# Small tensors allocated behind the large ones, so that every large matmul operand starts at a multiple of 256 bytes of SBUF

## The chip, the cores and the metric

One core of one Trainium2 chip runs the whole program in one launch. The metric is device time in microseconds, the median of a few runs; lower is better.

## What is computed

A decoder of two layers on x (2 sequences of 512 tokens, 512 features, float32), with a context of 2 x 1024 x 512. Each of six steps is a layer norm, a block, and an addition to the residual stream:

```python
x = x + L0_attn(ln(x))                  # causal self-attention, 16 heads of 32
x = x + L0_xattn(ln(x), ctx, mask)      # softmax(x ctx^T) ctx over 1024 context rows, no weights
x = x + L0_ffn(ln(x))                   # 16 experts, 6 per token, gated, inner 352; 2 shared
x = x + L1_attn(ln(x))                  # RMS norm, rotary, 32 query heads of 64 in 8 groups
x = x + L1_xattn(ln(x), ctx, ctx, ones) # linear attention: relu features, 16 heads
x = x + L1_ffn(ln(x))                   # 8 experts, 2 per token, inner 352; 1 shared
```

## The kernel before

**Stages.** `program` runs six stages in this order: `Attention` a0 (0 to about 255 us in the profile), `Memory` m (to 375), `Mixture` f0 (to 960), `Attention` a1 (to 1520), `Linear` lin (to 1780) and `Mixture` f1. Each has a method per engine (`sp`, `pool`, `act`, `dve`, `pe`) that writes that engine's instructions out by hand, with semaphore waits between them; no scheduler reorders anything.

**Precision.** A float32 product is made of three float32r matmuls. Each operand is kept as a high part and a low part (names end in H and L), and `product` (L147 to 155) issues high·high, high·low and low·high into one PSUM bank. So nearly all matmuls have one line, L153, and are told apart by their tiles: `bank<-YL,a_WH` has the stationary operand a_WH and the moving operand YL.

```python
for j, (a, b) in enumerate(((lh, rh), (lh, rl), (ll, rh))):
    m = pe.matmul(out, a, b, ...)   # a: stationary, up to 128 columns; b: moving, up to 512 columns
```

**The matmuls with 512 moving columns**, on which the prediction turns (stationary, then moving):

- a0 and a1, Q/K/V projections: weights `WH`/`WL`, normed activations `k.YH`/`k.YL` (12 in a row for each product of four blocks); output projection: `QH`/`QL` (attention's output), `WH`/`WL`; scores of a1 (L1000): `QH`/`QL`, `KH`/`KL`; attention times values: `VH`/`VL`, `PH`/`PL` (tile `PHL`).
- m, scores: `YH`/`YL`, context `CH`/`CL`; readout: `PH`/`PL`, context rows `RH`/`RL`.
- f0 and f1, down projection (`_pe_down`): hidden `HH`/`HL`, weights `DH`/`DL`, nine a row tile.
- lin, keys: `W1`, `CH`/`CL`; values: `CH`/`CL`, `W2`; queries: `W1`, `YH`/`YL`; query features: `F`, `KH`/`KL`; output: `kfH`/`kfL`, `W2`.

The up projections of f0 and f1 have 352 moving columns (`XH`/`XL` or `YH`/`YL` stationary, `UH`/`UL` moving), key features of lin 256 (`F` moving), and the rest of a1 and a0 128 to 384.

**Where tensors lie.** `k.sb` (L143) opens an SBUF tensor. Tensors are placed one behind the other in the order of the calls, each rounded up to 32 bytes of every partition; the first begins at byte 16512. Those of `program` and `constants` stay for good, those of a stage are closed by its `end`, and the next stage starts again at the same byte. Small tensors between large ones therefore set the start of all that follow. The slices that a matmul takes begin at multiples of 512 bytes (of 1408 in the up projections) from the tile's start, so with 512 columns an operand's start modulo 256 is that of its tile.

Of the kernel before, what the change touches and what calls it, by code (L numbers as in the profile page):

```python
# [6 lines left out]
F32R = mybir.dt.float32r  # L7
BF16 = mybir.dt.bfloat16
# [6 lines left out]
P = 128  # L15
B, T, D = 2, 512, 512
NTOK = B * T
NT = NTOK // P
TT = T // P
KD = D // P  # L20
SC = 1024
CT = SC // P
# [46 lines left out]
class Kernel:  # L69
# [18 lines left out]
    def constants(self, t):  # L88
# [3 lines left out]
        self.upto, self.full, self.number = self.sb("upto", [16, 16]), self.sb("full", [7]), self.sb("number", [64])  # L92
# [50 lines left out]
    def sb(self, name, shape, dt=F32, scope=None):  # L143
        return (scope or self.ctx).enter_context(self.nc.sbuf_tensor(name, [P] + list(shape), dt))
# [266 lines left out]
class Attention:  # L411
# [15 lines left out]
    def __init__(self, k, name, w_qkv, w_out, heads, qtiles, hd, rotary=None, rms=None):  # L427
# [4 lines left out]
        sb = lambda nm, shape, dt=F32: k.sb(f"{name}_{nm}", shape, dt, s)  # L432
# [13 lines left out]
        self.top, self.total, self.inv = (sb(x, [self.SLOTS, 4]) for x in ("top", "total", "inv"))  # L446
        self.f, self.g = ([sb(f"{x}{i}", [T], F32R)[:, :] for i in range(2)] for x in "fg")
        self.causal = sb("causal", [T], BF16)
        if rotary is None:
            self.zeros = sb("zeros", [D])  # L450
        self.norm = Norm(k, name, lambda nm, shape: sb(f"n_{nm}", shape),
# [598 lines left out]
class Memory:  # L1050
# [6 lines left out]
    def __init__(self, k, ctxT, ctx_rows, mask):  # L1057
# [3 lines left out]
        sb = lambda nm, shape, dt=F32: k.sb(f"m_{nm}", shape, dt, s)  # L1061
# [4 lines left out]
        self.mb, self.valid, self.ones = sb("mb", [B, SC], BF16), sb("valid", [B]), sb("ones", [P], BF16)  # L1066
        self.E = [sb(f"E{i}", [SC]) for i in range(2)]
        self.PH, self.PL = [sb(f"PH{i}", [SC], F32R) for i in range(2)], [sb(f"PL{i}", [SC], F32R) for i in range(2)]
        self.top, self.total = sb("top", [NT, 2]), sb("total", [NT, 2])
        self.nb, self.inv = sb("nb", [NT]), sb("inv", [NT])  # L1070
        self.norm = Norm(k, "m", lambda nm, shape: sb(f"n_{nm}", shape), banks=list(range(NT)))
# [283 lines left out]
class Mixture:  # L1355
# [13 lines left out]
    def __init__(self, k, name, w_up, w_down, routed, shared, gated, router, bias, top, freed, turn, apart=0):  # L1369
# [4 lines left out]
        sb = lambda nm, shape, dt=F32: k.sb(f"{name}_{nm}", shape, dt, s)  # L1374
# [16 lines left out]
        self.XH, self.XL = sb("XH", [KD, P], F32R), sb("XL", [KD, P], F32R)  # L1391
        self.gate = sb("gate", [INNER])
        self.HH, self.HL = sb("HH", [3, P], F32R), sb("HL", [3, P], F32R)
# [894 lines left out]
class Linear:  # L2288
# [4 lines left out]
    HN, HD, FD = 16, 32, 64  # L2293
    G, VA, NP = P // 32, 33, 8
    PAIRS = {5: (0, 1, 2), 6: (3, 4, 5), 7: (6, 7)}

    def __init__(self, k, t, free):
        self.k, self.t, self.free = k, t, free
        HN, HD, FD, VA, NP = self.HN, self.HD, self.FD, self.VA, self.NP
        self.scope = s = ExitStack()  # L2300
        sb = lambda nm, shape, dt=F32: k.sb(f"lin_{nm}", shape, dt, s)
# [10 lines left out]
        self.bq, self.bk, self.bv, self.bo = sb("bq", [KD]), sb("bk", [KD]), sb("bv", [D]), sb("bo", [D])  # L2312
        self.am = sb("am", [CT])
# [3 lines left out]
        self.kfH, self.kfL = ([sb(f"kf{x}{i}", [HN * FD], F32R) for i in range(2)] for x in "HL")  # L2317
        self.v = sb("v", [HN, VA])
        self.vHL = [sb(f"vHL{i}", [2, HN, VA], F32R) for i in range(2)]
        self.acc = sb("acc", [B * NP, 2 * VA])  # L2320
        self.zerob = sb("zerob", [3 * 4 * VA], BF16)
        self.kvH, self.kvL = sb("kvH", [B * NP, 2 * VA], F32R), sb("kvL", [B * NP, 2 * VA], F32R)
# [540 lines left out]
def program(nc, t):  # L2863
    with ExitStack() as ctx:
        k = Kernel(nc, t, ctx)
        k.X, k.stats = k.sb("X", [NT, D]), k.sb("stats", [NT, 6])
# [135 lines left out]
```

## Time and profile before

| what | value |
|---|---|
| median of 3 runs | 1956.21 us (1951.85 to 1958.1) |
| the profiled execution, first to last instruction (the page gives no other time of it) | 1968.5 us |
| its mean granted TensorE clock | 0.966 |
| busy: PE, PEld, DVE, ACT, POOL | 93%, 81%, 56%, 40%, 51% |
| chain that ended last: PE | 55% of the span |

PE is TensorE's matmuls, PEld its weight loads, which run beside the matmuls. Matmuls overlap: a row's duration is from issue to the modelled end, so a row of 390 ns can be followed by the next start after 230 ns. The spacing of the starts is what a matmul costs when PE is never idle. The granted clock is given as a share of full speed: 1.00 is the level of 2.4 GHz, 0.50 that of 1.2 GHz.

### The profile page before, as it was taken

How to read it: one execution, taken by the hardware profiler on the slowest of the kernel's cores; microseconds unless marked ns; L12 is line 12 of the kernel's file. 1: busy time of each engine (PE TensorE's matmuls, PEld its weight loads, DVE VectorE, ACT ScalarE, POOL GpSimd, SP SyncE). 2: the span in 40 equal slices, each digit the busy share in tenths (PEclk: the TensorE clock that was granted, in tenths of full speed). 3: DMA queues.
4: the chain of work that ended last, by engine and by line, in shares of the span. 5: the costliest groups of instructions: out<-in, count | busy, mean ns of one | idle time of the engine just before them, and what ended most of it. 6: DMA issues, size and time to landing. Idle time of an engine off the chain costs nothing.

```text
span 1968.5 us, 30804 instructions
## 1 busy us (share of the span) xinstructions
PE 1831.7 (93%) x10221; PEld 1597.7 (81%) x10221; DVE 1109.8 (56%) x2771; ACT 787.8 (40%) x2024; POOL 1008.5 (51%) x960
## 2 busy tenths in 40 slices
PE   7999989999899999999779999999999999998896
PEld 5888857778799999898568888888887888887785
DVE  5676785663333333336657666666665766445344
ACT  3766633212122222221356666666563433223231
POOL 3444342487864867885356456455443113016783
PEclk8999999999999999999889999999999999889898
DMA  3556431156554645553243233332331110012565
GB/s 110 164 159 199 136 134 44 46 183 229 190 177 127 212 153 181 173 162 107 73 104 102 67 90 95 85 90 66 93 100 39 34 49 22 1 45 95 191 209 187
DMA packets 102694, 232.33 MB, mean 118 GB/s; under 512 B 18816, under 2 KB 19072, under 8 KB 99472
## 3 DMA queue, kind: packets, MB, share of 16 engines
q1 hardware_dynamic: 82224, 144.11, 24.6%
q0 software_dynamic: 19744, 85.47, 13.2%
q8 instruction: 90, 1.47, 0.3%
q10 hardware_dynamic: 576, 0.79, 0.2%
q14 instruction: 60, 0.49, 0.1%
HBM read 126.23 MB, written 57.93 MB: 94 GB/s over the span
## 4 chain that ended last, share of the span: by engine, by line
PE 55%; POOL 5%; DVE 4%; issue 3%; DMA 3%; SPq 3%; ACT 2%; another core or an unknown queue 1%; POOLq 0%; DVEq 0%; ACTq 0%
PE bank L153 45%; PE bank L1016 2%; PE bank L1000 2%; SPq L669 2%; PE bank L2178 2%; DMA a_g<-a_f 2%; PE bank L2169 2%; POOL a_g L700 1%; DMA a_QL<-a_g 1%; POOL f_UL L165 1%; POOL a_E L706 1%; SPq L654 1%; PE bank L2788 1%; DVE X L1884 1%
## 5 line engine op out<-in xcount | busy, mean ns | idle before, releaser
L706 POOL TENSOR_SCALAR a_E<-a_E,a_inv 128x128 f32<-128x128 f32 (+3 forms) x384 | 220.5, 592 | 224.4 <-DVE a_inv L842 224.4
L153 PE MATMUL bank<-f_UH,f_XH 128*128 x596 | 201.7, 339 | 20.5 <-issue 11.6
L739 ACT ACTIVATE a_E<-a_E,a_top 128x512 f32<-128x512 f32 (+3 forms) x384 | 211.1, 567 | 6.5 <-DVE a_top L836 6.4
L153 PE MATMUL bank<-f_UH,f_XL 128*128 x596 | 193.9, 325 | 0.0
L153 PE MATMUL bank<-f_UL,f_XH 128*128 x596 | 193.7, 325 | 0.0
L731 ACT ACTIVATE a_PHL<-bank 128x512 fp32r<-128x512 f32 (+1 forms) x288 | 130.7, 528 | 133.5 <-PE bank L1016 133.4
L153 PE MATMUL bank<-a_PHL,a_VH 128*128 128x512 f32 (+3 forms) x768 | 180.8, 324 | 0.3 <-DVE a_QL L165 0.3
L836 DVE CUSTOM_DVE_ANT_0 a_E<-a_causal,bank 128x512 f32<-128x512 bf16 (+3 forms) x384 | 163.7, 481 | 29.9 <-PE bank L1000 18.2
L165 DVE TENSOR_TENSOR a_PHL<-bank,a_PHL 128x512 fp32r<-128x512 f32 (+1 forms) x288 | 153.7, 587 | 11.3 <-ACT a_PHL L731 11.1
L1772 ACT ACTIVATE f_HH<-bank 128x256 fp32r<-128x256 f32 x220 | 59.9, 325 | 240.5 <-PE bank L2169 217.3
L1827 DVE TENSOR_TENSOR f_gate<-bank,f_gate 128x352 f32<-128x352 f32 x79 | 41.3, 523 | 201.3 <-PE bank L153 172.2
L700 POOL TENSOR_TENSOR a_g<-a_g,a_cos_sin 128x512 f32<-128x512 f32 x40 | 70.7, 1768 | 158.1 <-DMA a_g<-a_f 158.1
L153 PE MATMUL bank<-f_DH,f_HH 128*128 (+1 forms) x330 | 139.5, 423 | 9.2 <-issue 6.2
L153 PEld LDWEIGHTS bank<-a_PHL,a_VH 128*128 128x128 f32 x768 | 134.8, 189 | 15.1 <-DVE a_QL L165 0.6
L165 POOL TENSOR_TENSOR f_UL<-f_uraw,f_UH 128x2816 fp32r<-128x2816 f32 (+1 forms) x27 | 141.5, 5241 | 2.3
L1016 PE MATMUL bank<-ident,a_E 128*128 128x128 f32 x960 | 126.3, 275 | 15.1 <-DVE a_PHL L165 9.5
L153 PE MATMUL bank<-YH,a_WH 128*128 128x512 f32 x288 | 123.3, 428 | 11.7 <-ACT a_f L809 7.2
L153 PEld LDWEIGHTS bank<-f_UH,f_XH 128*128 128x128 f32 x596 | 113.7, 191 | 23.1 <-issue 23.1
L153 PE MATMUL bank<-f_DH,f_HL 128*128 (+1 forms) x330 | 132.1, 400 | 0.0
L153 PE MATMUL bank<-f_DL,f_HH 128*128 (+1 forms) x330 | 131.3, 398 | 0.0
L165 POOL TENSOR_TENSOR f_DL<-f_draw,f_DH 128x1024 fp32r<-128x1024 f32 (+1 forms) x54 | 98.2, 1836 | 62.9 <-DVE f_row L217 60.8
L1016 PEld LDWEIGHTS bank<-ident,a_E 128*128 128x128 f32 x960 | 106.9, 141 | 22.1 <-DVE a_PHL L165 12.0
(397 smaller groups left out, 4951.4 us busy)
## 6 DMA issues: line engine op xcount, KB each, us to landing
f_uraw<-f_up POOLq DMA_DIRECT2D x18, 1408.0 KB
f_xb<-table SPq DMA_DIRECT2D x86, 256.0 KB
table<-f_ob SPq DMA_DIRECT2D x86, 256.0 KB
table<-a_zeros SPq DMA_DIRECT2D x31, 512.0 KB, 4.5
f_draw<-f_down POOLq DMA_DIRECT2D x27, 512.0 KB
a_g<-a_f SPq DMA_DIRECT2D x160, 64.0 KB, 2.0
a_raw<-a_qkv SPq DMA_DIRECT2D x36, 256.0 KB, 3.2
f_uraw<-f_up POOLq DMA_DIRECT2D x9, 704.0 KB
```

Source lines behind the costliest of these rows:

```text
L153: m = pe.matmul(out, a, b, start=first and i == 0 and j == 0, stop=last and i == n - 1 and j == 2, skip_group_check=not check)
L165: return dve.tensor_tensor(lo, src, hi, ALU.subtract)
L669: e.dma_start(self.g[s][32 * i:32 * i + 32, :].bitcast(F32), self.f[s][32 * (i ^ 1):32 * (i ^ 1) + 32, :].bitcast(F32)).then_inc(*self.s_t ...
L700: e.tensor_tensor(g, g, self.cos_sin[:, 1, :], ALU.mult).then_inc(*self.s_p2.up(N, *x))
L706: e.tensor_scalar(self.E[sl][:, a], self.E[sl][:, a], self.inv[:, sl, i:i + 1], 0.0, ALU.mult, ALU.add).then_inc(*self.s_nrm.up(N, m - 1, i))
L731: e.activation(self.PH[m % 2][:, at:at + size], bank[:, 0:size], ACT.Copy).then_inc(*self.s_phi.up(N, m - 2, ci))
L739: x = e.activation(E, E, ACT.Exp, scale=-1.0, bias=self.top[:, sl, i:i + 1], accum_out=self.total[:, sl, i:i + 1])
L836: e.tensor_tensor_reduce(self.E[sl][:, self.E_AT[i]:self.E_AT[i] + w], self.causal[:, T - w:T], bank[:, off:off + w], -1.0, HUGE, ALU.add, ...
L1000: t = e.matmul(bank[:, off:off + w], (self.QH, self.QL)[h][:, r, qs], keys[:, h, ks], start=x == 0, stop=x == 1)
L1016: t = e.transpose(self.k.bank[bk][:, at:at + P], self.E[sl][:, self.E_AT[i] + sblk * P:self.E_AT[i] + (sblk + 1) * P], self.k.ident[:, :])
L1772: m = e.activation(self.HH[ps, cs, :], src, ACT.Copy)
L1827: e.tensor_tensor(self.gate[:, :], bank[4 + n % 2][:, 0:INNER], self.gate[:, :], ALU.mult).then_inc(*self.s_hid.up(N, n))
```

## The change

Only the order of the `sb` calls changes, and one unused tensor (`to_line`, 160 bytes) is added. `full` moves from `constants` to the head of `program`, beside `stats` and in front of `X`; `Memory` opens the four row buffers of its norm itself, in front of its small tensors. Every engine's instructions, their order and their waits are the same row for row, apart from line numbers and one tile's name (`m_n_y` becomes `m_y`). What changes is the start of the tensors, modulo 256 bytes:

| tiles | before | after |
|---|---|---|
| `X` | 128 | 0 |
| `YH`, `YL`, `ident`, `identb` | 64 | 0 |
| a0, a1: `WH` `WL` `QH` `QL` `KH` `KL` `QS` `KS` `VH` `VL` `E` `PHL` | 96 | 0 |
| m: `CH` `CL` `RH` `RL` | 96 | 0 |
| m: `E`, `PH`, `PL` | 128 | 0 |
| f0, f1: `UH` `UL` `DH` `DL` `XH` `XL`, `xb`, `ob`, rows | 96 | 0 |
| f0, f1: `HH`, `HL` | 224 | 0 |
| lin: `W1` `W2` `F` | 96 | 0 |
| lin: `CH` `CL` `KH` `KL` `kf` `kfH` `kfL` | 192 | 0 |
| lin: `kvH`, `kvL` | 160, 32 | 0, 128 |
| lin: `vHL0`, `vHL1` | 0, 128 | 0, 128 |

```diff
@@ -89,7 +89,7 @@
 
         e = self.pool
         self.ones, self.earlier = self.sb("ones", [P], BF16), self.sb("earlier", [P], BF16)
-        self.upto, self.full, self.number = self.sb("upto", [16, 16]), self.sb("full", [7]), self.sb("number", [64])
+        self.upto, self.number = self.sb("upto", [16, 16]), self.sb("number", [64])
         self.s_zeros, self.s_cleared, s_ones = self.event("zeros"), self.event("cleared"), self.event("ones")
         self.s_zeros.plan(())
         tiles = (6 * NTOK + 16 * (P - 1)) // P
@@ -443,11 +443,11 @@
         self.E = [sb(f"E{i}", [1280]) for i in range(self.SLOTS)]
         PHL = sb("PHL", [4, 1280], F32R)
         self.PH, self.PL = [PHL[:, i, :] for i in range(2)], [PHL[:, 2 + i, :] for i in range(2)]
-        self.top, self.total, self.inv = (sb(x, [self.SLOTS, 4]) for x in ("top", "total", "inv"))
         self.f, self.g = ([sb(f"{x}{i}", [T], F32R)[:, :] for i in range(2)] for x in "fg")
         self.causal = sb("causal", [T], BF16)
         if rotary is None:
             self.zeros = sb("zeros", [D])
+        self.top, self.total, self.inv = (sb(x, [self.SLOTS, 4]) for x in ("top", "total", "inv"))
         self.norm = Norm(k, name, lambda nm, shape: sb(f"n_{nm}", shape),
                          [self.E[i][:, a * D:(a + 1) * D] for i in range(self.SLOTS) for a in range(2)], rms)
         self.head_rows = [(h, slice(h * hd, h * hd + hd)) for h in range(heads)]
@@ -1063,12 +1063,13 @@
         self.CH, self.CL = sb("CH", [KD, SC], F32R), sb("CL", [KD, SC], F32R)
         self.RH, self.RL = sb("RH", [CT, D], F32R), sb("RL", [CT, D], F32R)
         self.ma, self.mf = sb("ma", [B, SC], U8), sb("mf", [SC])
-        self.mb, self.valid, self.ones = sb("mb", [B, SC], BF16), sb("valid", [B]), sb("ones", [P], BF16)
+        self.mb, self.ones = sb("mb", [B, SC], BF16), sb("ones", [P], BF16)
         self.E = [sb(f"E{i}", [SC]) for i in range(2)]
         self.PH, self.PL = [sb(f"PH{i}", [SC], F32R) for i in range(2)], [sb(f"PL{i}", [SC], F32R) for i in range(2)]
-        self.top, self.total = sb("top", [NT, 2]), sb("total", [NT, 2])
+        y = [sb(f"y{i}", [D])[:, :] for i in range(4)]
+        self.top, self.total, self.valid = sb("top", [NT, 2]), sb("total", [NT, 2]), sb("valid", [B])
         self.nb, self.inv = sb("nb", [NT]), sb("inv", [NT])
-        self.norm = Norm(k, "m", lambda nm, shape: sb(f"n_{nm}", shape), banks=list(range(NT)))
+        self.norm = Norm(k, "m", lambda nm, shape: sb(f"n_{nm}", shape), y, banks=list(range(NT)))
         sig = lambda x: k.event(x, "m")
         self.s_mask, self.s_c0, self.s_c1, self.s_r = map(sig, ("mask", "c0", "c1", "r"))
         self.s_ones, self.s_mf, self.s_mb, self.s_clo_pool, self.s_rlo_pool = map(
@@ -1389,8 +1390,8 @@
         self.xb, self.ob = ([x[:, i * D:(i + 1) * D] for i in range(n)] for x, n in ((xb, self.XB), (ob, self.OB)))
         self.scratch, self.taken = {"early": xb, "late": ob}, {"early": 0, "late": 0}
         self.XH, self.XL = sb("XH", [KD, P], F32R), sb("XL", [KD, P], F32R)
+        self.HH, self.HL = sb("HH", [3, P], F32R), sb("HL", [3, P], F32R)
         self.gate = sb("gate", [INNER])
-        self.HH, self.HL = sb("HH", [3, P], F32R), sb("HL", [3, P], F32R)
         self.rw, self.RH, self.RL = sb("rw", [KD, R]), sb("rh", [KD, R], F32R), sb("rl", [KD, R], F32R)
         self.bs, self.sc, self.den = sb("bs", [R]), sb("sc", [NT, R]), sb("den", [NT])
         self.chosen = sb("chosen", [NT + 1, R], BF16)
@@ -2309,17 +2310,17 @@
         self.raw = sb("raw", [KD, D])
         self.FR = {x: sb(f"FR{x}", [self.G * FD]) for x in "kq"}
         self.F = {x: (sb(f"F{x}H", [self.G * FD], F32R), sb(f"F{x}L", [self.G * FD], F32R)) for x in "kq"}
-        self.bq, self.bk, self.bv, self.bo = sb("bq", [KD]), sb("bk", [KD]), sb("bv", [D]), sb("bo", [D])
-        self.am = sb("am", [CT])
+        self.bv, self.bo = sb("bv", [D]), sb("bo", [D])
         self.CH, self.CL = sb("CH", [KD, SC], F32R), sb("CL", [KD, SC], F32R)
         self.KH, self.KL = sb("KH", [KD, T], F32R), sb("KL", [KD, T], F32R)
         self.kf = sb("kf", [HN * FD])
         self.kfH, self.kfL = ([sb(f"kf{x}{i}", [HN * FD], F32R) for i in range(2)] for x in "HL")
+        self.vHL = [sb(f"vHL{i}", [2, HN, VA], F32R) for i in range(2)]
+        self.kvH, self.kvL = sb("kvH", [B * NP, 2 * VA], F32R), sb("kvL", [B * NP, 2 * VA], F32R)
+        self.acc = sb("acc", [B * NP, 2 * VA])
         self.v = sb("v", [HN, VA])
-        self.vHL = [sb(f"vHL{i}", [2, HN, VA], F32R) for i in range(2)]
-        self.acc = sb("acc", [B * NP, 2 * VA])
         self.zerob = sb("zerob", [3 * 4 * VA], BF16)
-        self.kvH, self.kvL = sb("kvH", [B * NP, 2 * VA], F32R), sb("kvL", [B * NP, 2 * VA], F32R)
+        self.bq, self.bk, self.am = sb("bq", [KD]), sb("bk", [KD]), sb("am", [CT])
         self.qfH, self.qfL = (c[:, :, :].rearrange("p k (a t) -> p (k a) t", t=T) for c in (self.CH, self.CL))
         self.den = sb("den", [2, HN])
         self.o = [self.kf[:, i * D:(i + 1) * D] for i in range(2)]
@@ -2863,7 +2864,8 @@
 def program(nc, t):
     with ExitStack() as ctx:
         k = Kernel(nc, t, ctx)
-        k.X, k.stats = k.sb("X", [NT, D]), k.sb("stats", [NT, 6])
+        k.stats, k.full, _ = k.sb("stats", [NT, 6]), k.sb("full", [7]), k.sb("to_line", [40])
+        k.X = k.sb("X", [NT, D])
         k.YH, k.YL = k.sb("YH", [KD, NTOK], F32R), k.sb("YL", [KD, NTOK], F32R)
         k.ident, k.identb = k.sb("ident", [P]), k.sb("identb", [P], BF16)
         s_in = [k.event(f"x_in{i}") for i in range(4)]
```

## Rows read from the trace of the kernel before

**Rows 1.** Page, engine: busy us, share of the span, instructions

```profile
PE 1831.7 (93%) x10221; PEld 1597.7 (81%) x10221; DVE 1109.8 (56%) x2771; ACT 787.8 (40%) x2024; POOL 1008.5 (51%) x960
```

**Rows 2.** Table by stretch, columns as in its head

```profile
core 0: us, PE busy (x) PEld busy (x) DVE busy (x) ACT busy (x) POOL busy (x), PEclk, DMA share, GB/s
...
255.00:375.00 120.00, 112.56 (x524) 86.56 (x525) 80.94 (x142) 38.72 (x80) 37.89 (x23) 0.97 0.21 77
375.00:960.00 585.00, 552.34 (x3193) 502.40 (x3192) 248.91 (x557) 129.50 (x323) 417.20 (x289) 0.98 0.50 163
960.00:1520.00 560.00, 525.17 (x2947) 456.13 (x2946) 361.85 (x1024) 329.20 (x911) 288.04 (x352) 0.98 0.32 83
1520.00:1780.00 260.00, 249.95 (x1359) 215.77 (x1358) 157.91 (x289) 83.42 (x138) 35.82 (x26) 0.92 0.11 34
...
965.00:968.30 3.30, 3.30 (x9) 2.53 (x9) 0.67 (x2) 0.00 (x0) 0.00 (x0) 0.50 0.00 0
```

**Rows 3.** Chain of waits, shares by line: 375:960, 960:1520, 1520:1780

```profile
by line: PE bank L153 56.7%; PE bank L2178 3.6%; PE bank L2169 3.3%; POOL f_UL L165 3.2%; issue 2.9%; POOL table L1601 2.0%; another core or an unknown queue 1.8%; DVE X L1884 1.3%; POOL f_UH L1719 1.3%; POOL f_DL L165 0.6%; PE bank L349 0.
...
by line: PE bank L153 41.1%; PE bank L1016 7.0%; PE bank L1000 6.9%; SPq L669 6.2%; DMA a_g<-a_f 5.6%; POOL a_g L700 4.6%; issue 4.3%; DMA a_QL<-a_g 3.7%; POOL a_E L706 3.1%; SPq L654 2.8%; ACT a_f L809 1.8%; DVE a_f L884 1.6%; DVE a_E L836
...
by line: PE bank L153 76.0%; PE bank L2788 6.0%; PE bank L2790 3.7%; PE bank L349 2.3%; PE bank L2838 2.1%; DVE lin_CL L2633 1.3%; issue 1.1%; POOL lin_CL L165 1.0%; PE bank L140 0.8%; DVE lin_KL L162 0.6%; ACT lin_KH L2538 0.5%; DVE lin_kv
```

**Rows 4.** Groups of PE, whole span (busy us, mean ns, idle us)

```profile
L153 PE MATMUL bank<-YH,a_WH 128*128 128x512 f32 x288 | 123.3, 428 | 11.7 <-ACT a_f L809 7.2
...
L153 PE MATMUL bank<-f_DH,f_HH 128*128 (+1 forms) x330 | 139.5, 423 | 9.2 <-issue 6.2
...
L153 PE MATMUL bank<-m_CH,YH 128*128 128x512 f32 x64 | 27.3, 426 | 1.1 <-DVE YL L165 1.1
...
L153 PE MATMUL bank<-lin_CH,lin_W1H 128*128 128x512 f32 x64 | 27.0, 421 | 5.0 <-issue 2.7 <-DVE lin_CL L165 2.3
```

**Rows 5.** Timeline of PE, output projection of a1: start, duration, instruction

```profile
1074.47 0.39 PE L153 MATMUL bank<-a_WH,a_QH 128*128 128x512 f32 x1
...
1077.19 0.39 PE L153 MATMUL bank<-a_PHL,a_VH 128*128 128x512 f32 x1
```

**Rows 6.** Timeline of PE, scores of Memory

```profile
329.16 0.40 PE L153 MATMUL bank<-m_CH,YH 128*128 128x512 f32 x1
...
331.96 0.39 PE L1340 MATMUL bank<-m_mb,m_ones 128*128 128x512 bf16 x1
```

**Rows 7.** Timeline of PE, Q/K/V projections, granted clock 0.50

```profile
965.12 0.63 PE L153 MATMUL bank<-YH,a_WH 128*128 128x512 f32 x1
...
967.68 0.63 PE L153 MATMUL bank<-YH,a_WH 128*128 128x512 f32 x1
```

**Rows 8.** Groups of PE by shape, 1024 to 1459, granted clock 1.00

```profile
L153 PE MATMUL bank<-YL,a_WH 128*128 128x512 f32 x160 | 63.1, 395 | 0.0
...
L153 PE MATMUL bank<-a_WL,a_QH 128*128 128x512 f32 x96 | 37.4, 390 | 0.0
...
L153 PE MATMUL bank<-a_PHL,a_VL 128*128 128x512 f32 x55 | 21.4, 389 | 0.0
...
L1000 PE MATMUL bank<-a_KL,a_QL 128*128 128x512 f32 x28 | 11.0, 392 | 0.0
```

**Rows 9.** The same from 522 to 790: f0, granted clock 1.00

```profile
L153 PE MATMUL bank<-f_DL,f_HH 128*128 x80 | 31.5, 394 | 0.0
...
L153 PE MATMUL bank<-f_DH,f_HL 96*128 x40 | 16.0, 401 | 0.0
```

**Rows 10.** Groups of PE with 352 and 256 columns

```profile
L153 PE MATMUL bank<-f_UH,YL 128*128 128x352 f32 x160 | 52.1, 325 | 0.0
...
L153 PE MATMUL bank<-f_UH,f_XL 128*128 x596 | 193.9, 325 | 0.0
...
L153 PE MATMUL bank<-lin_FkL,lin_KH 128*128 128x256 f32 x32 | 9.0, 280 | 0.0
...
L153 PE MATMUL bank<-a_PHL,a_VL 128*128 128x256 f32 x55 | 15.5, 282 | 0.0
```

**Rows 11.** Groups of ACT, PSUM to SBUF, 128x512

```profile
L759 ACT ACTIVATE a_QH<-bank 128x512 fp32r<-128x512 f32 x40 | 23.8, 596 | 35.6 <-PE bank L153 35.6
...
L2545 ACT ACTIVATE lin_CH<-bank 128x512 fp32r<-128x512 f32 x16 | 9.6, 599 | 2.1 <-PE bank L153 1.2
```

## The prediction

> **What bounds the kernel now.** I read the page's busy times first. PE is busy 1831.7 of 1968.5 us, no other engine more than 56% [rows 1]. The table by stretch says the same of every stage: in m PE is busy 112.56 of 120 us, in f0 552.34 of 585, in a1 525.17 of 560, in lin 249.95 of 260 [rows 2]. The chain of waits runs through PE too, but not everywhere alike: L153 alone is 76.0% of it in lin and 56.7% in f0, in a1 41.1% with another 14% on L1016 and L1000, the rest on the rotary's DMAs, on POOL and on queues [rows 3]. So this is a kernel whose end is set by how fast PE streams columns, and the change adds, removes and moves no instruction. It can only act through the time that one instruction takes. The question is therefore whether any duration in this trace depends on where its operands start.
>
> **What depends on the start.** Before the change the large tiles start at five different places modulo 256 (64, 96, 128, 192 and 224), so the trace holds the comparison already. I took matmuls of one shape (128 rows, 128x512 float32r), back to back, with the clock fully granted, and read the spacing of their starts.
>
> - Output projection of a1, weights and moving operand both in tiles at 96: twelve starts from 1074.47 to 1077.19, 226.7 ns each [rows 5].
> - Scores of m, stationary at 64, moving at 96: twelve starts from 329.16 to 331.96, 233.3 ns each [rows 6].
>
> The group means, which hold issue to modelled end, differ by as much: 390 ns for the output projection, 389 for attention times values and 392 for the scores of a1, all with both operands at 96; 395 for the projections, whose activations lie at 64 and weights at 96 [rows 8]; 394 and 401 in f0's down projection, stationary at 224, moving at 96 [rows 9]. Moving or stationary alone doesn't sort them (YH at 64 as moving operand gives 395, as stationary one 233.3 ns of spacing, the same class). What sorts them is whether the two starts agree modulo 256. I call these pairs in step and out of step. At a granted clock of 0.50 out-of-step pairs are spaced by 2.56 us over six, 426.7 ns, which is 512 columns at 1.2 GHz and nothing more [rows 7, 2]. So what is lost at full speed, 233.3 against 213.3 for 512 columns at 2.4 GHz, is time in which the operands come too slowly.
>
> The Trainium skill speaks against any of this. Its page "SBUF — State Buffer" gives PE two read ports, one for the moving operand and one for the weights, independent of each other (section "Who interferes with whom"), and says of its rule on operand starts that it is about legality, not speed (section "Operand start alignment"). If the two reads never meet, the sum below is 0; the 226.7 and 233.3 ns above speak against that.
>
> **The change part by part.**
>
> 1. Price of one out-of-step pair brought into step. From above: 233.3 - 226.7 = 6.6 ns. From the means: 395 - 390 = 5 ns; the least difference is 394 against 392 = 2 ns, the greatest 401 against 389 = 12 ns [rows 5, 6, 8, 9]. I take 5 ns, the middle of the group means, since not every in-step run reaches 226.7.
> 2. How many. Projections of a0 and a1: 288 of `YH`·`WH`, three matmuls for each, 864. Down projections: 330 x 3 = 990. m: 64 x 3 for the scores and, by the loops, as many for the readout, 384. lin: 64 x 3 each for keys and values, and half as many each for queries and output, a quarter for the query features, 624 [rows 4]. Together 2862. At 5 ns that is 14.3 us of PE time: 4.3 in a0 and a1, 5.0 in f0 and f1, 1.9 in m, 3.1 in lin.
> 3. How much of it reaches the end. Where PE is busy all the time a saved nanosecond is one of the span, unless PE then waits for something else. In lin the lines of PE hold 90% of the chain: 3.1 x 0.9 = 2.8. In m I take the busy share, 0.94: 1.8. In f0 and f1 between the chain's share of L153 and the transposes (64%) and the busy share (94%), 0.8: 4.0; POOL, which splits the experts' weights, is late next, at 417 of 585 us. In a0 and a1 between 55% and 94%, 0.72: 3.1; the rotary's DMAs and POOL's share of it don't shrink [rows 2, 3]. Sum 11.7 us.
> 4. Matmuls that don't gain. The up projections take 325 ns with 352 columns whether the stationary operand is `YL` (64 against 96 or 224) or `f_XL` (in step or half a row off): their step doesn't matter, and most keep theirs [rows 10]. Output projections, attention times values and a1's scores are in step and stay so. Key features of lin, 256 columns, may lose: out of step 280, while the in-step ones of a1 take 282 [rows 10]; 64 x 3 x 2 ns = 0.4 us.
> 5. The other engines. ACT's 128x512 evictions take 596 ns into a tile at 96 and 599 into one at 192 [rows 11]. I price ACT, DVE and POOL at 0; the two bound it at 0.5% of one instruction's time, either way.
> 6. DMAs keep number, size and order. The rows I read hold no pair of like DMAs at two starts. The rotary's a_g<-a_f and a_QL<-a_g are 9.3% of a1's chain, 52 us [rows 3]; a twentieth on them would be 2.6 us either way, which goes to the range. I take 0, as nothing here shows a dependence.
>
> Sum: 11.7 - 0.4 = 11.3 us of the profiled execution's 1968.5. That execution is 0.6% over the median of the runs, 1956.21, so the sum is 11.2 us of the median, and the forecast 1945 us.
>
> **The rivals.**
>
> - *Nothing arrives.* Either the 6.6 ns belong to something else that these groups don't share (their PSUM bank, their place in the program), or the saved PE time comes back as waits: a1's scores, transposes and softmax already wait for each other, and POOL's split of weights could take over in f0. For it: 392 ns of a1's scores, in step, is close to the 394 of f0. Against it: three in-step families agree at 389 to 392, and 395 recurs in three stages. Time 1956, give or take 4. Chance 18%. The Trainium skill's rule of two independent ports ("SBUF — State Buffer", above) ends at this time as well.
> - *In step is the wrong step.* All in-step pairs in this trace start at 96. If a start at a 256-byte boundary for both makes their reads meet in the same place each time, every changed pair could go to the highest level seen, 401 where 395 is usual now [rows 8, 9]: 2862 x 5 ns x 0.8 = 11.4 us; the pairs already in step, some 900 in output projections, values and a1's scores, would go the same way, 3.6 us. Time 1971. It decides where in-step pairs go above 395. For it: the 256-column pairs, 282 in step against 280. Against it: all in-step rows with 512 columns. Chance 8%.
> - *The start itself costs, too.* 96 is not a multiple of 64. If a start at 0 also takes away the 13.4 ns that even in-step pairs lose (226.7 - 213.3), all large matmuls gain, not the 2862 alone: about 3800 with 512 columns and 2300 with 352, at 13.4 ns and 0.8, 65 us. Time 1891. For it: the loss vanishes at half clock, so it is one of supply. Against it: `YH` at 64 is no faster as a moving operand than `CH` at 96 is. Chance 8%.
>
> That the change doesn't do what it says is no rival here: the built program has the starts of the table.
>
> **How the numbers follow.** The likeliest case, pairs in step at 226.7 to 229, has 66% and gives 1945, from 1938 (6.6 ns and nine tenths through) to 1952 (2 ns). A measurement here tells about 0.3% from no change, 5.9 us, so faster by over that means below 1950.3. From the first case 0.58 lies there, from the second 0.02, from the last 0.08: faster 0.68. Within 0.3%: 0.08 of the first and 0.14 of the second, 0.22. Slower: 0.02 of the second and the third rival, 0.10. The range 1928 to 1962 takes in the first two cases with a DMA term of 2.6 us either way and some of a partial gain from the starts; it leaves out most of the two rivals with 8% each.
>
> **What would show it.** In the profile after, the means of `YL`·`WH`, `m_CL`·`YH`, `f_DH`·`f_HL` and `lin_CL`·`W1H` at full clock should fall from 394 to 401 to about 390, spacings from 233 to 227, while the output projection stays at 390, the 352-column groups at 325, and ACT's evictions at 596. PE's busy time falls by 11 to 19 us. If the means fall and the span doesn't, PE's waits in a1 and f0 have grown by as much. If the output projection's 390 moves, the start itself counts, and the third rival, or with the other sign the second, is at work. If no mean moves, the sorting by steps was wrong.

## Result and profile after

| kernel | runs | median | ratio to before, 95% interval |
|---|---|---|---|
| before | 6 | 1955.66 us (1949.2 to 1959.1) | 1 |
| the change | 6 | 1944.63 us (1943.59 to 1946.79) | 0.9948 [0.9934, 0.9962] |

The change is faster by 0.52%, 10.2 us of 1955.66, between 7.4 and 12.9 by the interval. The forecast was 1945.0, from 1928 to 1962.

The busy times of the page after; before they read 1831.7 for PE [rows 1]. PE's 6 missing records (10215 of 10221) are lost records, not lost work.

```profile
PE 1816.0 (93%) x10215; PEld 1594.2 (82%) x10221; DVE 1110.1 (57%) x2771; ACT 787.2 (40%) x2024; POOL 1007.8 (52%) x960
```

PE has changed by 15.7 us and its weight loads by 3.5 (PEld, 1597.7 before [rows 1]); DVE, ACT and POOL agree to 0.8 us. But not all of the 15.7 is the change's. The profiled execution of before was 12 us longer than the median of its runs. A copy of the kernel before was profiled again beside the experiments (run control_before below), and its table by stage, cut at the first instruction of a0, m, f0, a1, lin and f1, reads:

```profile
core 0: us, PE busy (x) PEld busy (x) DVE busy (x) ACT busy (x) POOL busy (x), PEclk, DMA share, GB/s
0.00:255.50 255.50, 230.27 (x1306) 197.53 (x1306) 179.50 (x570) 154.51 (x445) 102.03 (x167) 0.96 0.49 153
255.50:373.80 118.30, 112.13 (x513) 85.65 (x513) 78.75 (x138) 37.73 (x79) 37.14 (x22) 0.96 0.21 76
373.80:953.70 579.90, 545.49 (x3186) 499.07 (x3186) 248.57 (x550) 128.92 (x317) 414.15 (x287) 0.98 0.50 164
953.70:1514.20 560.50, 526.13 (x2953) 457.55 (x2953) 361.21 (x1019) 331.11 (x919) 288.41 (x354) 0.98 0.32 82
1514.20:1774.50 260.30, 250.26 (x1350) 216.31 (x1350) 158.23 (x299) 82.39 (x137) 37.03 (x28) 0.92 0.11 36
1774.50:1956.40 181.90, 160.06 (x916) 139.02 (x916) 84.23 (x200) 54.00 (x130) 127.77 (x105) 0.97 0.56 184
sum 1956.40, PE 1824.33 PEld 1595.13 DVE 1110.49 ACT 788.67 POOL 1006.52; mean PE 304.05 PEld 265.86 DVE 185.08 ACT 131.44 POOL 167.75
```

Cut in the same way, the last stage of the first profile of before is

```profile
1776.10:1968.50 192.40, 164.82 (x916) 141.94 (x916) 84.25 (x200) 54.00 (x130) 127.90 (x105) 0.94 0.54 174
```

10.5 us longer than in the second, with a granted clock of 0.94 in place of 0.97: that is where its 12 us lie, and no layout explains them, since the two kernels are the same. The table of the changed kernel, the same columns:

```profile
0.00:254.20 254.20, 230.40 (x1307) 197.61 (x1307) 179.53 (x570) 153.76 (x445) 102.47 (x167) 0.96 0.49 154
254.20:370.80 116.60, 110.28 (x508) 85.67 (x514) 78.80 (x138) 37.82 (x79) 37.09 (x22) 0.96 0.21 76
370.80:948.10 577.30, 547.12 (x3185) 501.26 (x3185) 248.55 (x550) 128.76 (x317) 414.54 (x287) 0.98 0.50 165
948.10:1509.10 561.00, 525.21 (x2953) 457.98 (x2953) 360.96 (x1019) 330.58 (x919) 288.68 (x354) 0.98 0.32 82
1509.10:1762.50 253.40, 243.29 (x1350) 212.85 (x1350) 158.01 (x299) 82.25 (x137) 37.09 (x28) 0.93 0.11 37
1762.50:1944.00 181.50, 159.67 (x916) 138.82 (x916) 84.28 (x200) 54.02 (x130) 127.89 (x105) 0.97 0.55 185
sum 1944.00, PE 1815.97 PEld 1594.19 DVE 1110.12 ACT 787.18 POOL 1007.76; mean PE 302.66 PEld 265.70 DVE 185.02 ACT 131.20 POOL 167.96
```

Against the control PE has lost 8.4 us and the span 12.4. Most of it is in lin, 6.9 us, where PE has lost 7.0; f0 and m follow with 2.6 and 1.7, a0 with 1.3, a1 has nothing. The experiments show how far such a table of one execution can be believed: not to 3 us.

The matmuls themselves: scores of m, which were spaced by 233.3 ns [rows 6], twelve starts from

```profile
327.22 0.39 PE L153 MATMUL bank<-m_CH,YH 128*128 128x512 f32 x1
...
329.71 0.39 PE L153 MATMUL bank<-m_CH,YL 128*128 128x512 f32 x1
```

2.49 us over eleven, 226.4 ns, the level of the output projection [rows 5]. These twelve follow the readout, now in step too, without a break. The next dozen begins anew and does not come to that level; its starts 2 to 12 go by 231 ns (2.31 us over ten):

```profile
330.39 0.39 PE L153 MATMUL bank<-m_CL,YH 128*128 128x512 f32 x1
...
332.70 0.39 PE L153 MATMUL bank<-m_CH,YL 128*128 128x512 f32 x1
```

The groups from 1024 to 1459, which were 395, 390 and 392 [rows 8], are 394, 390 and 393:

```profile
L153 PE MATMUL bank<-YL,a_WH 128*128 128x512 f32 x160 | 63.0, 394 | 0.0
...
L153 PE MATMUL bank<-a_WL,a_QH 128*128 128x512 f32 x104 | 40.6, 390 | 0.0
...
L1000 PE MATMUL bank<-a_KL,a_QL 128*128 128x512 f32 x27 | 10.6, 393 | 0.0
```

The 394 is not the level of the projections at full clock. In this execution the granted clock was 0.50 between 1027.5 and 1030, and two of the 160 rows took 0.63 us, one of them

```profile
1029.44 0.63 PE L153 MATMUL bank<-YL,a_WH 128*128 128x512 f32 x1
```

From 1031 to 1450, where the clock was at 1.00, the mean is 391, 4 ns less than before:

```profile
L153 PE MATMUL bank<-YL,a_WH 128*128 128x512 f32 x158 | 61.7, 391 | 0.0
```

Of f0, 522 to 790, where 394 and 401 stood [rows 9]:

```profile
L153 PE MATMUL bank<-f_DL,f_HH 128*128 x79 | 30.9, 391 | 0.0
...
L153 PE MATMUL bank<-f_DH,f_HL 96*128 x40 | 15.8, 396 | 0.0
```

These two fell, but the 96-row `f_DL`,`f_HH` of the same stretch rose from 392 to 395, and the spacing of the nine hardly moved (next table).

ACT's evictions stay at 596 and 598 [rows 11]:

```profile
L759 ACT ACTIVATE a_QH<-bank 128x512 fp32r<-128x512 f32 x40 | 23.8, 596 | 34.8 <-PE bank L153 34.8
...
L2546 ACT ACTIVATE lin_CH<-bank 128x512 fp32r<-128x512 f32 x16 | 9.6, 598 | 1.9 <-PE bank L153 1.2
```

**The spacing by family.** For the next table all pairs of consecutive starts within a family, at a granted clock of 1.00 and less than 260 ns apart, were averaged from the starts in the trace (38 to 790 pairs each). "Offset" is the start of the moving operand less that of the stationary one, modulo 256.

| family, matmuls | offset before | control_before | the change | saved |
|---|---|---|---|---|
| Q/K/V projections, 864 | 224 | 232.9 ns | 229.5 ns | 2.9 us |
| m, scores, 192 | 32 | 233.2 | 229.2 | 0.8 |
| m, readout, 192 | 224 | 232.9 | 227.6 | 1.0 |
| lin, keys, 192 | 96 | 233.5 | 227.5 | 1.2 |
| lin, values, 192 | 160 | 234.2 | 228.5 | 1.1 |
| lin, queries, 96 | 224 | 233.1 | 227.1 | 0.6 |
| lin, output, 96 | 160 | 233.9 | 228.9 | 0.5 |
| lin, query features, 48 | 96 | 234.6 | 227.5 | 0.3 |
| lin, key features (256 columns), 192 | 160 | 117.8 | 119.8 | -0.4 |
| f0, f1, down projections, 990 | 128 | 233.1 | 232.5 | 0.6 |
| output projections (in step in both) | 0 | 228.4 | 228.4 | 0 |

The sum is 8.6 us, as much as PE's busy time lost against the control (8.4) and within the interval of the time. It is an estimate: it counts matmuls at half clock as if they gained too, though projections out of step and in step are spaced by 426.7 and 426.6 ns there, and it leaves out attention times values with 512 columns, which follow the projections. Those are in step in both kernels and still went from 229.4 to 227.5 ns, 0.5 us over 288. Three eighths of the 8.6 are lin's, a third the projections'. The 990 down projections, the dearest term of the prediction, give almost nothing.

### The profile page after: what moved, and what is told of

Read it like the earlier page. It is cut to its first block and busy times, and to the rows that moved or that the text cites. A ratio compares the mean times of both kernels' runs of the same rounds, so it can differ in the third digit from the quotient of the medians.

```text
span 1944.0 us, 30798 instructions
## 1 busy us (share of the span) xinstructions
PE 1816.0 (93%) x10215; PEld 1594.2 (82%) x10221; DVE 1110.1 (57%) x2771; ACT 787.2 (40%) x2024; POOL 1007.8 (52%) x960
## 5 line engine op out<-in xcount | busy, mean ns | idle before, releaser
L1773 ACT ACTIVATE f_HH<-bank 128x256 fp32r<-128x256 f32 x220 | 59.8, 325 | 232.6 <-PE bank L2170 232.5
L153 PEld LDWEIGHTS bank<-a_PHL,a_VH 128*128 128x128 f32 x768 | 135.1, 189 | 14.3 <-DVE a_QL L165 0.6
```

The costliest lines, as they stand in the source:

```text
L153: m = pe.matmul(out, a, b, start=first and i == 0 and j == 0, stop=last and i == n - 1 and j == 2, skip_group_check=not check)
L1773: m = e.activation(self.HH[ps, cs, :], src, ACT.Copy)
```

## Experiments

**control_before, all_at_96, y_at_32, hidden_at_128.** The first is a copy of the kernel before. The second is the change with 96 bytes more in front, so that every operand starts at 96 and all stay in step:

```diff
-        k.stats, k.full, _ = k.sb("stats", [NT, 6]), k.sb("full", [7]), k.sb("to_line", [40])
+        k.stats, k.full, _ = k.sb("stats", [NT, 6]), k.sb("full", [7]), k.sb("to_line", [64])
```

The third is the change with `YH` and `YL` alone moved to 32 (the tensors behind them stay), the fourth the change with `HH` and `HL` at 128:

```diff
+        k.sb("y_from", [8])
         k.YH, k.YL = k.sb("YH", [KD, NTOK], F32R), k.sb("YL", [KD, NTOK], F32R)
+        k.sb("y_to", [56])
```

```diff
-        self.HH, self.HL = sb("HH", [3, P], F32R), sb("HL", [3, P], F32R)
         self.gate = sb("gate", [INNER])
+        self.HH, self.HL = sb("HH", [3, P], F32R), sb("HL", [3, P], F32R)
```

Expected of control_before:

> The kernel before, unchanged, profiled a second time, to tell what of the two profiles' 24.5 us is the change and what is the execution. Step theory (spacing alone): the spacings repeat to 0.5 ns (projections 233, readout of m 233, values of lin 233 to 235), but the stage f1, 192.4 us in the first profile of before and 181.5 in that of the change, is nearer to 185 here, since its nine-matmul products hardly changed their spacing; median time within 0.2% of before. Rival (f1 itself gained from the layout, for instance in its transfers): f1 is again 190 to 194 us.

Expected of all_at_96:

> The changed kernel with 96 bytes more in front of X: every large operand starts at 96 modulo 256 and no longer at 0, and all pairs stay in step with each other. Step theory: spacings as in the change (projections 229 to 231, readout of m 227, keys and values of lin 227 to 229), time 1944 to 1947 us. Rival (the start itself counts): spacings between the two kernels or back at 233, time 1948 to 1956 us; if transfers to tiles at 96 are slower, f0 and f1 are longer by several us with unchanged spacings.

Expected of y_at_32:

> The changed kernel with YH and YL alone moved by 32 bytes, all else at 0: the projections of a0 and a1, the scores of m and the queries of lin are out of step again, 864 + 192 + 96 matmuls with 512 columns. Step theory: their spacings return to 232 to 234 (from 227 to 231), readout of m and values of lin stay at 227 to 229; PE time 1152 x 4 ns = 4.6 us more, time 1947 to 1949 us. Rival (start, not step): only YH's own reads are touched, at most a change of 1 ns, time 1944 to 1946 us.

Expected of hidden_at_128:

> The changed kernel with HH and HL behind gate again: in f0 and f1 the hidden tiles start at 128 modulo 256 against 0 for the down weights, half a row off as before the change. Step theory with a settling time (a product of nine never settles): the down projections' spacing moves by less than 1.5 ns from 231 to 234 (990 matmuls, less than 1.5 us), time 1944 to 1947 us. Rival (my forecast for these, 5 ns each): f0 and f1 are 4 to 5 us longer together, time 1948 to 1950 us.

| run | median | ratio to before, 95% interval | projections | m scores | lin queries | down |
|---|---|---|---|---|---|---|
| control_before | 1954.74 us | 0.9999 [0.9987, 1.0011] | 232.9 ns | 233.2 | 233.1 | 233.1 |
| all_at_96 | 1944.75 | 0.9951 [0.9934, 0.9969] | 229.7 | 229.4 | 226.8 | 232.4 |
| y_at_32 | 1950.26 | 0.9974 [0.9962, 0.9986] | 233.1 | 232.7 | 233.4 | 232.3 |
| hidden_at_128 | 1943.96 | 0.9947 [0.9931, 0.9962] | 229.5 | 229.2 | 226.7 | 233.1 |

all_at_96 has the time and the spacings of the change: where operands start does not matter, only how they stand to each other. The multiple of 256 in the change's description is not the cause. y_at_32 takes about half of the gain away, 5.1 us by the ratios (its time, 1950.26 us, lies above the expected 1947 to 1949). The three families with `Y` go back, and their spacings give 3.1 + 0.7 + 0.6, 4.4 us; readout, keys and values of lin stay in step (227.8, 227.5 and 228.5 ns). But three families that hold no `Y`, and are in step here as in the change, go up as well: attention times values from 227.5 to 231.2 ns, the scores of a1 from 230.3 to 233.4, lin's query features from 227.5 to 232.0. They come behind matmuls with `Y`; the last section returns to them. hidden_at_128 puts the 990 down projections out of step again and costs nothing that the time shows: 233.1 ns against 232.5. That term of the prediction had failed, and the next runs ask why.

**y_at_64, y_at_128: how fine is the step?** As y_at_32, with 16 words in front of `YH` and 48 behind `YL`, or 32 and 32:

```diff
+        k.sb("y_from", [16])
         k.YH, k.YL = k.sb("YH", [KD, NTOK], F32R), k.sb("YL", [KD, NTOK], F32R)
+        k.sb("y_to", [48])
```

Expected of y_at_64:

> YH and YL at 64, all else at 0 as in the change, so 1152 pairs (864 projections of a0 and a1, 192 scores of m, 96 queries of lin) are 64 bytes out of step. What is out of step at 32 bytes was spaced by 232.2 to 233.6 ns. If any difference below 256 bytes counts (my theory, and before had 64 against 96): the same 232 to 234 ns for YL,a_WH, m_CL,YH and YL,lin_W1H, time some 5 us above the change, 1950. Rival, that a pair is in step when the starts agree modulo 64: 227 to 230 ns and the change's time, 1944.6. One look: the spacings decide, not the time.

Expected of y_at_128:

> YH and YL at 128, all else at 0. If the step is a whole 256 bytes: 232 to 234 ns for the 1152 pairs, time some 5 us above the change. Rival, that it is 128 bytes (half a step already counts as in step): 227 to 230 ns and the change's time, 1944.6. One look: the spacings decide.

One run each: 1948.42 and 1950.67 us beside 1955.75 for before. Groups of y_at_64, projections from 1024 to 1459 and scores of m:

```profile
L153 PE MATMUL bank<-YL,a_WH 128*128 128x512 f32 x160 | 62.6, 391 | 0.0
...
L153 PE MATMUL bank<-m_CL,YH 128*128 128x512 f32 x64 | 25.3, 396 | 0.0
```

and of y_at_128, the projections from 1034 to 1450, where its clock was at 1.00

```profile
L153 PE MATMUL bank<-YL,a_WH 128*128 128x512 f32 x157 | 61.8, 394 | 0.0
...
L153 PE MATMUL bank<-m_CL,YH 128*128 128x512 f32 x64 | 25.2, 394 | 0.0
```

At 128 all three families are out of step (232.3, 232.7 and 232.4 ns): the step is not 128 bytes, nor 64. At 64 neither expectation held whole. Scores, with the stationary operand 64 ahead, are at 233.7, but projections and queries, with the moving one 64 ahead, are at 229.6 and 229.7, as good as in step for the projections. So the direction seems to count, which no theory had. It is not shown apart from the family, since no run has one family at both 64 and 192; at 32, 128 and 224 the three agree to 0.7 ns whichever operand is ahead. With the offsets of the other runs every multiple of 32 has been seen for 512 columns:

| offset | 0 | 32 | 64 | 96 | 128 | 160 | 192 | 224 |
|---|---|---|---|---|---|---|---|---|
| ns | 226.7 to 230.0 | 233.1 to 233.4 | 229.6, 229.7 | 233.4 to 234.9 | 232.3 to 232.7 | 233.4 to 234.2 | 233.7 | 232.7 to 233.4 |

(The lowest and highest mean of a family in any run. Left out are the down projections, which are the next point, and three families in step of which the last section tells: lin's query features, and the values and scores of a1, at 227.2 to 231.2 and 230.1 to 233.5 ns.) The readout of m, whose tiles differ by an odd multiple of 256 after the change, is at 227.6: 256 is enough, it need not be 512.

**down_twice_in_step, down_twice_out_of_step.** Each down projection issued twice into its bank, in the change and in the kernel before. What the hidden part adds counts double.

```diff
-        product(e, self.k.bank[bk][:, :], [(self.HH[0:rows, c, :], self.HL[0:rows, c, :])
...
-                 for c, (_, rows) in enumerate(ITILES)]).then_inc(*self.s_out.up(N, n))
+        hid = [(self.HH[0:rows, c, :], self.HL[0:rows, c, :]) for c, (_, rows) in enumerate(ITILES)]
+        wts = [(flat(self.DH[0:rows, buf, c, :]), flat(self.DL[0:rows, buf, c, :])) for c, (_, rows) in enumerate(ITILES)]
+        product(e, self.k.bank[bk][:, :], hid, wts, last=False)
+        product(e, self.k.bank[bk][:, :], hid, wts, first=False).then_inc(*self.s_out.up(N, n))
```

Expected of down_twice_in_step:

> The change with every down projection issued twice into the same bank (18 matmuls in a row where there were 9; the hidden part counts double, so the output is another one). HH, HL and DH, DL are in step. The theory on why the 990 down projections hardly gained (231.2 to 234.5 ns of spacing, as before): a run in step needs some six starts before it settles at 227, as the output projection's first ones do, and nine are over too soon. Then the starts 10 to 18 are at 226 to 228 ns here, and the mean of all falls to about 229.5. Rival: the down projections are slow for another reason (their 96-row slices, their operands' places), then the second nine show 231 to 235 ns as the first. Time about 330 x 9 x 9 / 9 x 0.23 = 330 x 9 / 3 x 0.23 us more PE work, some 220 us on 1944.6, about 2165.

Expected of down_twice_out_of_step:

> The kernel before with every down projection issued twice into the same bank (output another one, as in down_twice_in_step). Stationary at 224, moving at 96, out of step. By the theory of settling the second nine stay at 232 to 235 ns, and the whole is slower than down_twice_in_step by the change's 10 us and 990 x 5 ns, 5 us, more. Rival (another reason): first and second nine alike in both kernels, 231 to 235 ns, and the two kernels differ by 10 us only.

2149.44 and 2160.91 us, one run each: 11.5 apart. The run-up asked for some 15, the rival for 10; the two times don't decide it, the spacings do. The timeline of one product in step (start, duration, instruction), starts 2, 9 to 11 and 16 to 18, then the transposes behind:

```profile
605.36 0.39 PE L153 MATMUL bank<-f_DL,f_HH 128*128 x1
...
606.98 0.39 PE L153 MATMUL bank<-f_DH,f_HL 96*128 x1
607.21 0.39 PE L153 MATMUL bank<-f_DH,f_HH 128*128 x1
607.44 0.39 PE L153 MATMUL bank<-f_DL,f_HH 128*128 x1
...
608.57 0.40 PE L153 MATMUL bank<-f_DH,f_HH 96*128 x1
608.81 0.40 PE L153 MATMUL bank<-f_DL,f_HH 96*128 x1
609.04 0.39 PE L153 MATMUL bank<-f_DH,f_HL 96*128 x1
609.27 0.49 PE L2170 MATMUL bank<-ident,f_gate 128*128 128x128 f32 x3
```

Starts 2 to 10: 1.85 us over eight, 231 ns. Starts 11 to 16: 1.13 over five, 226 ns, the level. Starts 16 to 18 and on: 0.70 over three, 233 ns, and these are the matmuls with 96 rows. Averaged over 109 of the 110 products, the spacings behind starts 2 to 9 and 10 to 17 are, in ns:

```
in step        231 234 230 231 231 233 235 229 | 231 229 227 228 228 227 233 236
out of step    231 231 230 235 237 239 230 234 | 235 235 231 230 231 233 239 232
```

So in-step runs do need a run-up: over the first eight spacings the kernels differ by 1.6 ns (231.8 and 233.4 on average), over the second eight by 3.4 (229.9 and 233.3). The expected 226 to 228 came for four of those eight only. The same run-up stands in the output projection, in step in both kernels: after 0.41 us of idle time its starts in the changed kernel

```profile
1066.59 0.47 PE L153 MATMUL bank<-a_WH,a_QH 128*128 128x512 f32 x1 [0.41 <-DVE a_QL L165]
1066.89 0.39 PE L153 MATMUL bank<-a_WL,a_QH 128*128 128x512 f32 x1
...
1069.43 0.39 PE L153 MATMUL bank<-a_WH,a_QH 128*128 128x512 f32 x1
...
1070.79 0.39 PE L153 MATMUL bank<-a_WH,a_QH 128*128 128x512 f32 x1
```

go by 231 ns for eleven (2.54 us) and only then by 227 (1.36 over six). And it stands in the projections. Averaged over the dozens that ran at full clock throughout (66 in control_before, 65 in the change), the spacings behind starts 2 to 12 are, in ns:

```
control        232 232 233 232 231 234 232 234 232 234 233
the change     232 233 231 228 230 230 227 229 228 227 227
```

The first two gain nothing, the last five 4 to 7 ns. A run of nine behind transposes is over before most of that.

**y_only, lin_only, lin_undone, down_96_first.** Two halves of the change done alone on the kernel before, one undone in the change, and one try at the 96 rows. y_only adds the two lines of y_at_32 to the kernel before (`YH`, `YL` at 96). lin_only takes the change's lines of `Linear` alone, lin_undone is the change without them:

```diff
-        self.bv, self.bo = sb("bv", [D]), sb("bo", [D])
+        self.bq, self.bk, self.bv, self.bo = sb("bq", [KD]), sb("bk", [KD]), sb("bv", [D]), sb("bo", [D])
+        self.am = sb("am", [CT])
         self.CH, self.CL = sb("CH", [KD, SC], F32R), sb("CL", [KD, SC], F32R)
...
-        self.bq, self.bk, self.am = sb("bq", [KD]), sb("bk", [KD]), sb("am", [CT])
```
down_96_first sums the tiles of the hidden width in another order:

```diff
+        tiles = [(c, ITILES[c][1]) for c in (2, 0, 1)]
...
-                 for c, (_, rows) in enumerate(ITILES)]).then_inc(*self.s_out.up(N, n))
+                 for c, rows in tiles]).then_inc(*self.s_out.up(N, n))
```

Expected of y_only:

> The kernel before with 32 bytes in front of YH and 224 behind YL, so that YH and YL begin at 96 as the weights and contexts that they meet, and nothing else moves. 1152 pairs come into step: 864 projections of a0 and a1, 192 scores of m, 96 queries of lin. By the step: YL,a_WH from 233 to 228.5, m_CL,YH from 233 to 227, all other groups as before, and 1152 x 5 ns x 0.8 = 4.6 us, ratio 0.9976, the mirror of y_at_32, which gave back 5.5 us. Rival, that the gain comes from elsewhere and y_at_32 only cost something of its own: ratio 0.999 or more.

Expected of lin_only:

> The kernel before with the small tensors of lin alone moved behind its large ones: C, K, kf at 96 as W1, W2 and F. 528 pairs come into step (keys and values 384, output 96, query features 48), at the spacings seen in the change 232.8 to 227.8 and 235.9 to 227.2, about 6 ns each: 3.2 us, less 0.4 for the key features, 2.8 us, ratio 0.9986. Rival, that all of lin's 5.9 to 6.9 us by the stage table come from these pairs (through the clock too, which is at half for 34 to 37 us of lin in the change and for 41 to 44 before): ratio 0.997.

Expected of lin_undone:

> The change with lin's small tensors where they were: C, K, kf at 96, W1, W2, F at 0, so the same 528 pairs out of step again, at +96 and -96 as in the kernel before. By the step: lin's spacings back at 232.8 and 235.9, all else as in the change, the change's time and 2.8 us, ratio to before 0.9963. Rival (all of lin's gain): 0.998.

Expected of down_96_first:

> The change with the three tiles of the down projection's sum in another order: the 96-row one first, the two of 128 rows behind it (same sum). In the change the last two spacings of nine are 236 and 233 ns, and where the nine are issued twice the second nine run 231, 229, 227, 228, 228, 227 and then 233, 236: only the 96-row matmuls at the end leave the level. If it is the 96 rows: the slow pair stands at the front, and the last spacings are 227 to 230. Rival, that it is the end of a product (what comes next): the last two stay at 233 to 236. Time in any case within 1.5 us of the change, 1943 to 1946, ratio 0.994 to 0.9955.

| run | median | ratio to before, 95% interval | projections | lin keys, values | down |
|---|---|---|---|---|---|
| y_only | 1950.11 us | 0.9976 [0.9965, 0.9986] | 229.3 ns | 233.4, 234.0 | 233.1 |
| lin_only | 1950.74 | 0.9983 [0.9973, 0.9993] | 232.9 | 227.5, 228.7 | 233.1 |
| lin_undone | 1946.54 | 0.9965 [0.9952, 0.9978] | 229.6 | 233.4, 233.9 | 232.3 |
| down_96_first | 1942.48 | 0.9942 [0.9928, 0.9956] | 229.4 | 227.5, 228.5 | 230.9 |

y_only came out at the expected ratio, 4.7 us, the mirror of y_at_32. lin_only and lin_undone give lin's pairs 3.3 us each (from 0.9983, and from 0.9965 less 0.9948), near the 2.8 expected and not the 5.9 that the rival asked for; the rival's 0.997 and 0.998 lie outside both intervals. Their groups show values (512 columns) and key features (256) going opposite ways, lin_only first:

```profile
L153 PE MATMUL bank<-lin_W2L,lin_CH 128*128 128x512 f32 x64 | 25.0, 390 | 0.0
L153 PE MATMUL bank<-lin_FkL,lin_KH 128*128 128x256 f32 x64 | 18.1, 283 | 0.0
```

lin_undone:

```profile
L153 PE MATMUL bank<-lin_W2L,lin_CH 128*128 128x512 f32 x64 | 25.3, 395 | 0.0
L153 PE MATMUL bank<-lin_FkL,lin_KH 128*128 128x256 f32 x64 | 17.9, 280 | 0.0
```

What of the 6.9 us that lin lost in the table by stage? Some 3.3 us is spacing, by the table of families. The rest goes with the clock: worked out from the granted clock and the stage's length, lin ran 34.1 us at half speed in the change's execution and 44.3 in the control's, and half of these 10 us is lost, which alone would be more than the 3.6 us that are left. In the twelve other profiles it was 34.1 to 41.7, high and low in both layouts: 40.9 in lin_only, with keys and values in step, 34.1 in y_only, with both out of step. f0's 2.6 us are not shown to be the change's either: lin_only leaves all of f0 as it was, y_only all but the start of `Y`, and their f0 took 576.4 and 574.9 us, less than the change's 577.3. The row of lin_only:

```profile
373.00:949.40 576.40, 546.31 (x3186) 498.19 (x3186) 248.57 (x550) 128.80 (x317) 414.12 (x287) 0.98 0.50 165
```

One stage of one execution moves by 3 us and more by itself.

down_96_first brings the down projections from 232.5 to 230.9 ns, 1.6 us over 990, and has the lowest median of all. Its interval holds the change's ratio, so it is not shown to be faster. Its spacings behind starts 2 to 8 are 230, 229, 233, 234, 229, 231 and 230 ns, where the change has 234, 233, 234, 227, 231, 236 and 233. Neither expectation was met whole: the 96-row matmuls in front are not the slow ones, and the end of the product did not stay at 233 to 236. So 96 rows are slow only at the end; why is open.

## Why the prediction was right, and where it was not

1. *What depends on the start.* Right: it is the two operands' starts relative to each other, modulo 256 (with the one exception at an offset of 64, which the trace of before could not show). all_at_96 excludes the third rival (the start itself, 1891 us) and the second (in step as the wrong step, 1971): in step at 0 is as good as in step at 96. "Nothing arrives", 1956, is excluded by y_only and lin_only, which move one group each and gain what its spacings say. The Trainium skill's two independent read ports ("SBUF — State Buffer", section "Who interferes with whom") do not agree with 233.1 ns in y_at_32 and 229.5 in the change for the same projections, with the start of `Y` alone moved; here the measurement decides. Why the one start matters to the other no run shows.
2. *Price, 5 ns.* Right in size where runs are long: 3.4 for the projections, 4.0 and 5.3 in m, 5.0 to 7.1 in lin. The 6.6 ns at its upper side were the price of a settled matmul: the twelve output projections of [rows 5] are the second dozen of twenty-four in a row. The first dozen, in step as well, goes by 231 ns from

```profile
1071.93 0.39 PE L153 MATMUL bank<-a_WL,a_QH 128*128 128x512 f32 x1
```

to 1074.47 [rows 5], 2.54 us over eleven.
3. *Count, 2862 pairs, 14.3 us.* This is the step that failed. The 990 down projections were priced as the rest, 5.0 us; they gave 0.6. The price was taken from a settled stretch and from the means of longer runs, without asking whether nine behind transposes get to the level; [rows 9] showed 394 and 401 and was read as out of step alone. The projections were over-priced as well, 2.9 us for 4.3, for the same reason: each run pays for its run-up. m came to 1.8 for 1.9, lin to 3.7 for 3.1. Together 9.0 us in place of 14.3.
4. *What reaches the end, 11.7 of 14.3.* Too low by the medians, and this made up for most of step 3. y_only: spacings 4.1 us (864 x 3.6, 192 x 3.2, 96 x 3.8), measured 4.7 [2.7, 6.8]. lin_only: 2.5 and 3.3 [1.4, 5.3]. The change: 8.6 and 10.2 [7.4, 12.9]. By the prediction's own shares these spacings would have given 3.2, 2.2 and 7.2 us; the first two lie within the intervals and the third just outside. So it is likely, not shown, that more arrives than the prediction had; the chain's share of 41% in a1 [rows 3] then was no guide to what a faster matmul is worth there.
5. *Key features lose 0.4 us.* Right: 117.8 to 119.8 ns, 0.4 us. *Up projections don't move:* right, a median of 160 ns in both. *Output projections, values and a1's scores don't move:* right for the output projections, 228.4, and the scores, 230.6 and 230.3; the values came 1.9 ns closer, with their own operands in step before and after.
6. *Other engines and DMAs 0.* Right within what one execution shows: DVE 1110.5 and 1110.1, ACT 788.7 and 787.2, POOL 1006.5 and 1007.8; the rotary's a_g<-a_f and a_QL<-a_g land after a median of 2.0 and 2.4 us in the control, 2.0 and 2.3 in the change.

The lower end of the likeliest case was added up wrongly: 2862 x 6.6 ns x 0.9, less 0.4, is 16.6 us and gives 1940, not 1938.

The forecast, 11.2 us less, lies 1.0 us from the 10.2 of the ratio because an over-count of 5.3 met what was, by the medians, an under-count of what arrives. Its direction and mechanism rest on the experiments; its last digits are luck.

Of what was to show it, PE's fall of 11 to 19 us came on the page (15.7), but against the control it is 8.4; the means came to some 390 in m and lin (389 and 390) and in the projections (391 at full clock), not for the down projections (391 to 396).

Not tried: more starts of the weights against the moving operand in f0, and a down projection whose third tile has 128 rows.

## What to carry to other kernels

Where matmuls follow each other without gaps, compare the starts of both operands modulo 256 bytes before looking for anything grander: two tiles that meet in float32r matmuls of 512 columns belong at the same remainder, whichever it is, and small tensors belong behind them. Count only the matmuls in long runs (a dozen and more), and read the spacing of the starts; a mean duration counts only where the clock was at 1.00 throughout, since two rows at half clock among 160 hid 3 of the 4 ns by which the projections' mean had fallen. Take a second profile of the same kernel before any stage's difference of a few microseconds is believed.

## What the runs showed of the hardware that was not expected

- The offset seems to have a sign. With the moving operand 64 bytes ahead of the stationary one the projections and queries are at 229.6 and 229.7 ns, with the stationary one 64 ahead the scores of m are at 233.7, in one kernel (y_at_64).
- The in-step level has a run-up: eleven spacings of 231 ns behind an idle stretch before 227. As far as these runs tell, the spacing also depends on what ran just before. Two families have their own operands in step in every run and move all the same: attention times values, directly behind the projections, are at 229.4 ns in the control, 227.5 in the change, and 231.2, 231.0 and 230.5 with `Y` at 32, 64 and 128 (173 pairs each); the scores of a1, behind the values, are at 230.6, 230.3 and then 233.4, 233.5 and 232.3 (59 to 61 pairs). Likewise the query features of lin are in step in y_at_32 and y_at_64 and yet at 232.0 and 231.8 ns, behind queries that start elsewhere than the weights, and at 227.5 in the change, behind queries in step (38 pairs each). This was not tried by itself.
- With 256 columns the sign is turned: 117.8 to 118.0 ns at an offset of 160, 119.7 to 119.8 in step, in all fourteen profiles.
- Nothing gets to the 213.3 ns of 512 columns at 2.4 GHz at any of the eight offsets. The bfloat16 matmuls of 512 columns (`identb`, one tile as both operands) are spaced by 217 ns in both kernels (39 and 34 pairs), so most of the last 13 ns goes with something in which the two kinds differ; with what is open.
